# First attention: staging of three groups on GpSimd, and the values' products of two steps in one block

## What is computed

```python
qkv = x @ w_qkv.T
q, k, v = qkv[0], qkv[1], qkv[2]
q = _rms_norm(q, q_norm_w); k = _rms_norm(k, k_norm_w)
q, k = _rope(q, k, cos, sin)
attn = einsum('bhqd,bhkd->bhqk', q, k) * scale
attn = softmax(where(causal, -inf, attn), axis=-1)
out = einsum('bhqk,bhkd->bhqd', attn, v)
```

## Time and profile before

| | us |
|---|---|
| median of 3 runs | 1631.74 |
| lowest and highest run | 1629.95, 1634.58 |
| profiled execution, its own time | 1631.0 |
| its span, first to last instruction | 1629.2 |
| first V to last V (L807) | 67 to 588 |
| mean granted TensorE clock | 0.985 of 2.4 GHz |

### The profile page before, as it was taken

The page is one execution under the profiler, slowest core; times in us unless marked ns, Lnnn a source line. Parts: engine busy times, 40 slices in busy tenths (PEclk is TensorE's granted clock), DMA queues, the critical chain, the costliest instruction groups (busy, mean ns, idle before and its releaser), DMA issues.

```text
span 1629.2 us, 27834 instructions
## 1 busy us (share of the span) xinstructions
PE 1532.1 (94%) x8374; PEld 990.3 (61%) x8374; DVE 1271.5 (78%) x2584; ACT 948.4 (58%) x1602; POOL 837.6 (51%) x949
## 2 busy tenths in 40 slices
PE   6889999999999987779999999999999999999998
PEld 5456655565565566657667566566566566665565
DVE  7898887787678447678788888788888887878765
ACT  5355567757755664355655755655656656556653
POOL 3820000000001125669678788689699699698553
PEclk9899999999999998889999999999999999999999
DMA  2000000000000000000000000000000000000000
GB/s 66 1 1 1 1 1 1 1 2 1 1 1 1 1 13 13 1 13 1 1 13 1 1 13 2 13 1 1 13 1 1 13 1 1 1 1 1 1 7 20
DMA packets 13673, 9.40 MB, mean 6 GB/s; under 512 B 3744, under 2 KB 13536, under 8 KB 13536
## 3 DMA queue, kind: packets, MB, share of 16 engines
q1 hardware_dynamic: 13536, 7.63, 1.7%
HBM read 6.58 MB, written 1.05 MB: 5 GB/s over the span
## 4 chain that ended last, share of the span: by engine, by line
PE 62%; POOL 18%; DVE 11%; issue 5%; ACT 3%; DMA 0%; DVEq 0%; SPq 0%; ACTq 0%; POOLq 0%
PE ps L773 9%; PE ps L990 9%; PE ps L807 8%; PE ps L792 8%; PE ps L957 5%; PE ps L978 4%; POOL gs L1785 4%; PE ps L979 4%; PE ps L729 4%; POOL gsum L1786 3%; POOL z L631 3%; POOL onm L625 3%; POOL h_qk L1787 2%; DVE mxp L1406 2%; DVE den L1636 2%
## 5 line engine op out<-in xcount | busy, mean ns | idle before, releaser
L1263 ACT ACTIVATE pbuf<-ps 128x512 f32<-128x512 f32 x512 | 301.7, 600 | 166.2 <-PE ps L979 162.5
L1102 ACT ACTIVATE pbuf<-ps 128x1024 f32<-128x1024 f32 (+3 forms) x320 | 280.6, 897 | 192.0 <-PE ps L795 101.8
L1406 DVE TENSOR_REDUCE mxp<-ps 128x1 f32<-128x512 f32 (+2 forms) x432 | 280.2, 686 | 68.4 <-PE ps L773 52.6
L1636 DVE TENSOR_TENSOR den<-den,pbuf 128x1024 f32<-128x1024 f32 x224 | 310.5, 1386 | 1.9
L990 PE MATMUL ps<-pbuf,h_v 128*64 128x512 f32 x1024 | 247.9, 605 | 0.0
L773 PE MATMUL ps<-kM,qT 128*128 128x512 f32 (+3 forms) x640 | 231.7, 412 | 14.7 <-ACT kM L1083 7.6
L1588 DVE TENSOR_TENSOR gt<-ps,gate 128x320 f32<-128x320 f32 x384 | 180.8, 483 | 78.5 <-POOL h_v L1795 47.6
L1249 ACT ACTIVATE relu<-ps 128x512 f32<-128x512 f32 x256 | 152.2, 599 | 145.1 <-PE ps L957 113.1
L1609 DVE CUSTOM_DVE_ANT_0 relu<-ps,relu 128x512 f32<-128x512 f32 x256 | 174.4, 684 | 65.5 <-PE ps L957 56.3
L978 PE MATMUL ps<-q1T,k1T 128*128 128x512 f32 x512 | 214.5, 419 | 10.7 <-ACT pbuf L1263 9.2
L979 PE MATMUL ps<-q2T,k2T 65*128 65x512 f32 x512 | 203.4, 397 | 0.0
(11 more groups left out here) (258 smaller groups left out, 2712.5 us busy)
## 6 DMA issues: line engine op xcount, KB each, us to landing
wraw<-in_Wkv SPq DMA_DIRECT2D x16, 160.0 KB, 2.7
wraw<-in_Wq SPq DMA_DIRECT2D x8, 160.0 KB, 2.3
x<-in_x SPq DMA_DIRECT2D x4, 256.0 KB, 3.8
out<-x SPq DMA_DIRECT2D x4, 256.0 KB, 2.3
wqkv<-in_wqkvT SPq DMA_DIRECT2D x1, 192.0 KB, 3.7
masks<-in_masks SPq DMA_DIRECT2D x1, 128.0 KB, 4.7
dft<-in_dft SPq DMA_DIRECT2D x1, 128.0 KB, 2.2
wout<-in_Wo SPq DMA_DIRECT2D x2, 64.0 KB, 2.3
```

The costliest lines, as they stand in the source:

```text
L1102: nc.scalar.activation(pbuf0[:, u % NP0, :, off:CH], ps[:, b:b + 2, off:CH], ACT.Exp, scale=float(D0) ** -0.5).then_inc(s_exp, 1)
L1263: nc.scalar.activation(pbuf1[:, u % NP1, i, :], ps[:, i, :], ACT.Exp, scale=float(D1) ** -0.5).then_inc(s_exp1, 1)
L1406: v.tensor_reduce(mxp[:, i, h:h + n, b], sc.rearrange("p (h k) -> p h k", h=n), AX.X, ALU.max).then_inc(s_read0d, 1)
L1636: v.tensor_tensor(dn, dn, w, ALU.add).then_inc(s_den1, 1)
```

## The change

- `stage_keys` and `stage_queries` become helpers for any engine. Group 0 stays on DVE, groups 1 to 3 go to POOL: the keys right behind POOL's copy of the group's values, the queries at their own place of the list.
- V: the products of steps k-1 and k stand side by side, behind S item 2k+3, so V comes for every fourth S item.
- `stagev` has 9 columns for each head (8 values and the ones) instead of 32; POOL's memsets of the other 23 go, and DVE clears bank 6 once at the start. A `spare` tensor keeps the addresses behind where they were.
- `pbuf0` has eight homes instead of six.
- `K_SHARED` loses (0,2) and (0,3): ACT makes all four copies of them.

```diff
-NP0, NP1 = 6, 5
+NP0, NP1 = 8, 5
-K_SHARED = ((0, 2), (0, 3), (1, 0), (1, 1), (1, 2), (1, 3), (2, 0), (2, 1), (3, 0), (3, 1))
+K_SHARED = ((1, 0), (1, 1), (1, 2), (1, 3), (2, 0), (2, 1), (3, 0), (3, 1))
-        stagev = s0("stagev", [P, 2, NT, GH, 32])
+        stagev = s0("stagev", [P, 2, NT, GH, D0 + 1])
+        s0("spare", [P, 2 * NT * GH * (32 - D0 - 1) - 2 * 2 * CH])
...
-            k = u // 2 - 2
-            if u % 2 == 0 and 0 <= k < N0:
-                seq.append(("V", k))
+            if u % 4 == 1 and 0 <= u - 5 < 2 * N0:
+                k = (u - 5) // 2 + 1
+                seq += [("V", k - 1), ("V", k)]
...
+        def stage_keys(eng, order_after, g, tiles):
+            gk = qkv[:, tiles, D + 32 * g:D + 32 * (g + 1)].rearrange("p n (h d) -> p n h d", d=D0)
+            eng.tensor_copy(stagek[:, tiles, :, D0:2 * D0].bitcast(F32R), gk)
+            order_after(eng.tensor_copy(stagek[:, tiles, :, 0:D0].bitcast(F32R), gk))
+            return eng.tensor_tensor(stagek[:, tiles, :, 2 * D0:3 * D0], gk, stagek[:, tiles, :, 0:D0], ALU.subtract)
...
-                        mm = pe.matmul(ps[32 * h:32 * h + 32, ACC, off:CH], stagev[:, g % 2, jt, h, :],
+                        mm = pe.matmul(ps[32 * h:32 * h + D0 + 1, ACC, off:CH], stagev[:, g % 2, jt, h, :],
...
+            v.memset(ps[:, ACC, :], 0.0)
...
-                if kind == "stagek" and step[1]:
-                    dve.wait_ge(s_roped, 1)
-                    wait_turn(dve, ring0, ("k", step[1] - 1, NC - 1))
-                    stage_keys(step[1], slice(0, NT))
-                elif kind == "stageq" and step[1]:
-                    if step[1] >= 2:
-                        wait_turn(dve, ring0, ("q2", step[1] - 2, NC - 1))
-                    stage_queries(step[1], slice(0, NT))
-                elif kind == "k" and step[1:] in K_BY_DVE:
+                if kind == "k" and step[1:] in K_BY_DVE:
...
-                ins = g_.memset(stagev[:, b, :, :, D0 + 1:32].rearrange("p n h r -> p (n h) r"), 0.0)
...
                     g_.tensor_copy(stagev[:, g % 2, :, :, 0:D0], gv).then_inc(s_stagev, 1)
                     pool.wait_ge(s_stagev, g + 1)
+                    if g:
+                        wait_turn(pool, ring0, ("k", g - 1, NC - 1))
+                        stage_keys(g_, link, g, slice(0, NT)).then_inc(s_stagek, 1)
+                elif step[0] == "stageq" and step[1]:
+                    g = step[1]
+                    if g >= 2:
+                        wait_turn(pool, ring0, ("q2", g - 2, NC - 1))
+                    stage_queries(g_, link, g, slice(0, NT)).then_inc(s_stageq, 1)
```

More of the change, by code:

```diff
@@ L631, in by_expert, with stage_queries @@
                 eng.tensor_tensor(z[:, n], z[:, n], onm[:, i - 1], ALU.add).then_inc(s_z, 1)
+        def stage_keys(eng, order_after, g, tiles):
[3 more added lines that the diff above has]
+            return eng.tensor_tensor(stagek[:, tiles, :, 2 * D0:3 * D0], gk, stagek[:, tiles, :, 0:D0], ALU.subtract)
+        def stage_queries(eng, order_after, g, tiles):
+            gq = qkv[:, tiles, 32 * g:32 * (g + 1)].rearrange("p n (h d) -> p n h d", d=D0)
+            to = queries(g)
+            eng.tensor_copy(to[:, tiles, :, 2 * D0:3 * D0].bitcast(F32R), gq)
+            eng.tensor_copy(to[:, tiles, :, 0:D0].bitcast(F32R), gq)
+            order_after(eng.memset(to[:, tiles, :, 24:32 if g == 1 else 25], 0.0))
+            return eng.tensor_tensor(to[:, tiles, :, D0:2 * D0], gq, to[:, tiles, :, 0:D0], ALU.subtract)
         block = ctx.enter_context(nc.Block())
@@ L1347, in roots @@
                 return ins
[L1349 to L1363, removed]
             dve.wait_ge(s_pconst, 1)
@@ L1370, in _ @@
                 link(norm_and_rotate(v, link, first, tiles))
-                stage_keys(0, tiles)
-                stage_queries(0, tiles)
+                stage_keys(v, link, 0, tiles).then_inc(s_stagek, 1)
+                stage_queries(v, link, 0, tiles).then_inc(s_stageq, 1)
             for step in SEQ0:
                 kind = step[0]
-                if kind == "stagek" and step[1]:
-                    dve.wait_ge(s_roped, 1)
-                    wait_turn(dve, ring0, ("k", step[1] - 1, NC - 1))
-                    stage_keys(step[1], slice(0, NT))
-                elif kind == "stageq" and step[1]:
-                    if step[1] >= 2:
-                        wait_turn(dve, ring0, ("q2", step[1] - 2, NC - 1))
-                    stage_queries(step[1], slice(0, NT))
-                elif kind == "k" and step[1:] in K_BY_DVE:
+                if kind == "k" and step[1:] in K_BY_DVE:
                     _, g, c = step
@@ L1682, in _ @@
             for b in range(2):
-                g_.memset(stagev[:, b, :, :, D0:D0 + 1].rearrange("p n h r -> p (n h) r"), 1.0)
-                ins = g_.memset(stagev[:, b, :, :, D0 + 1:32].rearrange("p n h r -> p (n h) r"), 0.0)
+                ins = g_.memset(stagev[:, b, :, :, D0:D0 + 1].rearrange("p n h r -> p (n h) r"), 1.0)
             ins.then_inc(s_pconst, 1)
```

## The result

| | before | after |
|---|---|---|
| median, 13 runs of each on one chip, us | 1631.49 | 1636.46 |
| lowest and highest run | 1629.78, 1635.58 | 1632.99, 1638.57 |
| ratio, 95% interval | | 1.0024 [1.0016, 1.0032] |
| profiled execution, its own time | 1631.0 | 1633.9 |
| its span | 1629.2 | 1632.1 |

A forecast was written before the change was run, and what follows sets the result against it. PE was taken to bound the kernel from 107 to 540 us. Pairs -14.0, opening -0.5, a further -1.0 and the part up to 107 us -2.0 gave -17.5 us: 1614.2 for the median, range 1603 to 1627.

The forecast's parts named there:

- The pair's price: Two V's side by side on PE take 1.87 us to the next matmul, where two single ones take 2.00.
- what remains of the 0.33: First attention: each pair saves PE 0.33 us; after waits on other engines all pairs together gain 14.0 us.
- The end: S items 284 to 320, nine pairs without maxima: PE waits for ACT's exponents, +0.25 us a pair, 2 us lost.
- Group 1: Part up to 107 us, with POOL staging group 1's keys and queries: net -2 us, between -5 and +3.
- the sentence on `K_SHARED`: Up to 107 us: DVE spared 2.8 us, ACT takes 2.3 more, PE's transposition bank free 1.2 later for each chunk.
- Nine columns: V with 9 instead of 32 columns: length doesn't follow the columns, taken as zero, within 5 us either way.
- The relief of DVE in group 2: POOL's staging spares DVE 3.1 us in group 2, where it is 85% busy; counted as 1.0 us gained.
- The opening: DVE's first squares no longer wait for POOL's memsets of stagev: at most 0.7 us gained, 0.5 taken.
- A: Rival: PE blocks on exponents or ring banks between pairs, handoffs eat half their gain; gain 8 us, 1624; chance 0.20.
- C: Rival: late keys of group 1 (+3) and the tail (+4.5) against 7 us from the middle; 1631; chance 0.09.
- B: Rival: DVE was the true pace of the first 270 us, each microsecond spared counts; 1603; chance 0.08.
- D: Rival: with 9 of 32 columns in use V may no longer hold the full clock; 1640; chance 0.06.

The follow-up runs named there:

- e8: The kernel before with V in pairs and DVE's unmasked maxima taken over the first half of each score bank: 1616.01 us, ratio 0.9905, from two runs.
- e9: The kernel before with V single and DVE's unmasked maxima taken over the first half of each score bank: 1627.52 us, ratio 0.9975.
- e4: The kernel before with V in pairs and nothing else changed (six homes, 32 columns): 1634.25 us, ratio 1.0019.
- e2: The changed kernel with the staging of groups 1 to 3 back on DVE, pairs kept: 1634.07 us, ratio 1.0016.
- e12: The changed kernel with V at single places and key chunks (0,2) and (0,3) back in K_SHARED: 1630.7 us, ratio 0.9989.
- e1: The changed kernel with V back at its single places, all else kept: 1634.57 us, ratio 1.0007.
- e3: The changed kernel with key chunks (0,2) and (0,3) back in K_SHARED, pairs kept: 1635.27 us, ratio 1.0025.
- e11: The kernel before with key chunks (0,2) and (0,3) taken out of K_SHARED, copied by ACT alone: 1633.9 us, ratio 1.0007.
- e6: Kernel before with nine columns, eight homes, shorter opening, pairs in steps 48 to 123, POOL staging groups 2 and 3 only: 1624.17 us, ratio 0.9959.
- e13: The kernel before with nine columns, eight homes, shorter opening and pairs in steps 48 to 123, staging on DVE: 1626.29 us, ratio 0.9955.
- e10: The kernel before with V in pairs for steps 48 to 123 alone, singles elsewhere: 1626.6 us, ratio 0.9974.

## Why the prediction was wrong

**The pair's price was right.** 1.84 us with nine columns, 1.85 with 32, against 1.87 forecast, and in blocks of x16. It had been read from blocks of eight records of 64 columns; that sixteen narrower ones take the same is seen but not explained. In e8 against e9, where DVE has room, pairs gain 9.7 us from item 95 to 251, 0.25 for each of 39; forecast was 0.27.

**The step that failed is what remains of the 0.33 where DVE keeps pace.** The sum took 14.0 us gained by the pairs, and e4 measured 3 us lost: 17 of the 22.5 us by which the forecast missed. The forecast counted when the eighth maximum gets its bank, from the first maximum behind the pair on, and took DVE's idle time as 0.6 to 0.9 us. It did not count how little DVE has in hand when a V begins: the three banks held 1.0 us of reductions at 215.21 (0.31 left of one and 0.69 for the next). With a body of 1.84 and 0.53 until the first maximum can be read, 1.4 us of idle time is the result, and 1.38 was measured. A single V leaves 0.45, two of them 0.9. Before, DVE had 5.49 us of work in a cycle of 6.31 (items 43 to 95). PE's saving would have made that 5.98, but in e4 DVE has 5.30 of work and 1.18 of idle time, and their 6.49 us are the cycle.

| S items | pairs | forecast | e4 measured |
|---|---|---|---|
| 43 to 95 | 13 | -2.6 | +2.3 |
| 95 to 251 | 39 | -10.5 | -5.4 |
| 251 to 283 | 8 | -2.2 | +2.2 |
| 283 to 319 | 9 | +2.0 | +2.8 |

(Forecast: 6 pairs at 0.12 and 7 at 0.27 in the first row, 0.27 for each in the next two.) Between 95 and 251 half of the gain remains, 0.14 us a pair. That the other half, too, goes to the ring is argued from e8 and e9, which have 9.7 there. Why items 251 to 283 lose was not settled. DVE is busier there than the 78% that the forecast took for the whole stretch (51.45 of 61.17 us before, 84%), but with half maxima pairs lose 1.4 us there as well (e8 -1.5, e9 -2.9), so DVE's length isn't all of it.

**The end.** The mechanism was right, PE waits for exponents, and the size nearly so. The cycle was forecast at 5.1 and measured at 5.27 against 4.58. Nine such cycles would lose 6.2 us; 2.8 were lost where 2 were forecast, so more than half was filled. After loses 2.6 us here, and 4.8 with items 251 to 283.

**Group 1.** The forecast had this part at -2, with +3 as its bound. It was +4.0 at item 15. POOL's staging came out as forecast: e2 against after is 1.5 us, 1.3 had been named. What failed is the sentence on `K_SHARED`: it priced ACT's four copies as work beside other work and as a later transposition bank, and did not name the table load and the roots queued behind them on ACT. It also read ACT's share from the wrong stretch (3.9 of 20 us, 60 to 80 us), while the copies run from 49.5 on. Before, stretch 40 to 60 us, has ACT at 11.1:

```profile
40.00:60.00 20.00, 14.13 (x64) 8.72 (x63) 18.17 (x37) 11.12 (x15) 12.14 (x9) 0.98 0.00 0
```

That step is 2.7 us by e12 against e1, and less by the runs of e3 and e11. DVE's relief, counted as a gain, fell into its wait of 6.90 us.

**Columns and staging.** Nine columns were taken at zero within 0.06 either way, and are worth 0.02 for each V, 3.3 us in e12 from item 15 on. In after less of it counts: from item 15 to 319 after loses 1.0 and e4 2.0, since PE waits anyhow. The relief of DVE in group 2, taken as 1.0, is nil by e6 and e13. The opening was taken as 0.5; after stands at -0.3 at item 0, but so do kernels with the old opening at -0.2 (e4, e10), and no run shows its gain.

**The range.** The bounds of the prediction's own terms add up to 1599 to 1630, wider than the 1606 to 1622 that it gives as their spread; the result lies outside both. Under A, 268 us for 40 pairs are 6.7 each, not 6.5, which changes nothing.

**Rivals.** C, the wash, was nearest: late keys and the end against some 6 us of the middle is what happened, and it lacked the dense part's loss of 2.4, with which it would be at some 1634. A had the right direction in the wrong place: handoffs to DVE, not to ACT. B fell, since spared DVE work brought nothing: 22 us less of it gained 0.6 in e9. D fell: in after the clock is at 1.00 in every stretch from 107 to 590 us.

**What after is made of**, at its last S item: e12, which has all but the pairs and the copies, stands at -1.0; the copies bring it to e1's +1.7, and the pairs to +5.0. By the ratios the same steps are -0.11%, +0.18% and +0.17%. POOL's keys are within the first, 1.5 us by e2, made good by the columns. The last V starts 5.0 us later than before (593.0 and 588.0), as much as the medians differ; the span shows 2.9, since the unchanged part behind it is 2.1 shorter in this one profile.

## What to carry to other kernels

Joining two blocks of one engine saves its switching, but it doubles the time for which that engine feeds nobody. So read first how much work its consumer has in hand when the block begins, and join only where that, or the consumer's slack, covers the longer gap: here in steps 48 to 123, which gains 0.26% where all steps lose 0.19% (by e10 and e4). And work that is handed to an engine with idle time should be priced by what stands next in that engine's queue, not by its busy share: 1.2 us more of copies on ACT put POOL's rotation 1.7 us later, because the square roots stood behind them.

## What the runs showed of the hardware that was not expected

- A V of nine stationary columns in a 32-column tile takes 0.976 us, one of 32 columns 0.996, with the same 512 columns moving.
- In after the clock stood at 1.2 GHz for 10 us behind PE's idle time of 6.29 us (0.81 in 27 us), although PE was at work again from 97.8 us on. The length of the wait alone doesn't tell the loss: e12 waited for 5.23 us at that place and has 0.94, e1 for 4.14 and has 0.87. In e6, where PE waited for only 0.32 us at that place, the same stretch has 0.95:

```profile
80.00:107.00 27.00, 24.18 (x126) 13.39 (x128) 25.98 (x51) 14.01 (x17) 12.99 (x8) 0.95 0.00 1
```

- A DVE cast beside POOL's memset ends 0.28 us behind the memset's end, whenever it started: after 3.82 us in e2, where it began 0.03 us ahead of the memset, after 2.22 in the earlier trace rows, against 0.42 alone. The SBUF page of the Trainium skill (SBUF — State Buffer, Who interferes with whom) says that a VectorE cast, where it runs in a mode with two ports, and a GpSimd instruction block each other fully; the traces agree for the cast. Staging on POOL didn't pay even so: POOL's casts take 0.62 and its subtraction 1.25, DVE's 0.42 and 0.69.
